# The q parts of a batch spread over three partition blocks: one transfer with the repetition outermost, or three transfers of 24 rows

## The reference, cut to what matters

```
q, k, v = heads of x @ W + b              # 8 batches, 16 heads, 512 rows, 8 dims
scores  = q @ k.T (* scale, + causal mask or bias)
p       = softmax(scores)
out     = (p @ v) joined over heads @ Wo + bo
```

## Time and profile before

| | us |
|---|---|
| median of 3 runs | 3335.12 |
| the runs | 3351.07, 3335.12, 3327.49 |
| span of the profiled execution | 3373.5 |
| TensorE busy in it | 2663.6 |
| layer 0's attention | about 0 to 620 |
| layer 0's experts and layer 1 | 620 to 1840 |
| layer 2 | 1840 to 2510 |
| layer 3 | 2510 to 3373.5 |

### The profile page before, as it was taken

The page is one execution under the profiler, slowest core; times in us unless marked ns, Lnnn a source line. Parts: engine busy times, 40 slices in busy tenths (PEclk is TensorE's granted clock), DMA queues, the critical chain, the costliest instruction groups (busy, mean ns, idle before and its releaser), DMA issues. The chain is left out here.

```text
span 3373.5 us, 52446 instructions
## 1 busy us (share of the span) xinstructions
PE 2663.6 (79%) x16466; PEld 1658.5 (49%) x16466; DVE 1628.8 (48%) x4008; ACT 1230.2 (36%) x2253; POOL 579.8 (17%) x594
## 2 busy tenths in 40 slices
PE   3777777788884788888888587877876888888887
PEld 1344444487772556556677243333443444444443
DVE  5566566400002444434423666666645555555553
ACT  1333333444443222222122244444432454444554
POOL 4322222000005433333100311111000000000000
PEclk7888888999996777777989698899888999999999
DMA  3112211266662000000054111111112011110111
GB/s 106 55 52 62 67 64 58 80 194 186 193 190 62 19 17 16 18 16 14 4 172 154 47 53 50 50 50 49 40 41 58 20 41 42 44 40 23 31 38 31
DMA packets 117431, 214.47 MB, mean 64 GB/s; under 512 B 21000, under 2 KB 90160, under 8 KB 110256
## 3 DMA queue, kind: packets, MB, share of 16 engines
q1 hardware_dynamic: 104048, 186.88, 18.5%
q0 software_dynamic: 10240, 20.99, 2.2%
q10 hardware_dynamic: 2880, 3.28, 0.3%
HBM read 158.50 MB, written 51.40 MB: 62 GB/s over the span
## 5 line engine op out<-in xcount | busy, mean ns | idle before, releaser
L525 DVE TENSOR_REDUCE arena<-bank 128x1 f32<-128x512 f32 (+3 forms) x1216 | 752.5, 658 | 221.7 <-PE bank L515 95.7
L501 PE MATMUL bank<-arena 125*128 125x512 bf16 (+3 forms) x1536 | 487.6, 357 | 174.1 <-DVE arena L525 107.1
L594 ACT ACTIVATE arena<-bank 128x512 f32<-128x512 f32 x640 | 378.9, 596 | 570.8 <-PE bank L584 506.6
L572 PE MATMUL bank<-arena 128*128 128x512 bf16 (+3 forms) x1536 | 469.1, 348 | 62.6 <-DMA arena<-arena 46.3
L594 ACT ACTIVATE arena<-bank,arena 128x512 f32<-128x512 f32 x512 | 343.3, 687 | 358.3 <-PE bank L572 249.0
L501 PEld LDWEIGHTS bank<-arena 125*128 125x128 bf16 x1536 | 146.2, 104 | 458.7 <-DVE arena L525 293.3
L609 PE MATMUL bank<-arena 128*32 128x512 f32 (+3 forms) x3072 | 318.8, 508 | 45.4 <-ACT arena L594 33.2
L572 PEld LDWEIGHTS bank<-arena 128*128 128x128 bf16 x1536 | 136.0, 103 | 285.3 <-ACT arena L594 130.5
L617 DVE COPY arena<-bank 128x512 f32<-128x512 f32 x96 | 66.4, 692 | 341.2 <-PE bank L609 330.8
L1023 POOL DMA_INDIRECT back_rows<-sorted_out,back_now x160 | 154.1, 963 | 404.1 <-issue 358.1
L1881 DVE TENSOR_TENSOR arena<-bank,arena 128x512 f32<-128x512 f32 (+3 forms) x256 | 109.8, 484 | 211.4 <-PE bank L1741 205.5
(11 more groups left out here) (250 smaller groups left out, 3667.9 us busy)
## 6 DMA issues: line engine op xcount, KB each, us to landing
arena<-in_L_ffn_w SPq DMA_DIRECT2D x80, 578.0 KB, 4.0
arena<-k_parts SPq DMA_DIRECT2D x48, 576.0 KB
arena<-q_parts SPq DMA_DIRECT2D x48, 576.0 KB
arena<-in_L_ffn_w SPq DMA_DIRECT2D x24, 768.0 KB, 4.5
arena<-sorted_in SPq DMA_DIRECT2D x104, 128.0 KB, 2.5
sorted_out<-arena SPq DMA_DIRECT2D x104, 128.0 KB, 4.1
k_parts<-arena SPq DMA_DIRECT2D x24, 384.0 KB
q_parts<-arena SPq DMA_DIRECT2D x72, 128.0 KB
```

Of the source, the lines that this page charges most:

```text
L501: ins = pe.matmul(mx[:, k * w:(k + 1) * w], Qx[0:KMAX, h, q * P:(q + 1) * P], Kx[0:KMAX, h, 0:w], start=(k == 0 or not L.causal), stop=not ...
L525: dve.reduce_max(L.mx[:, g % 2, q, heads[0]:heads[-1] + 1], mx[:, 0:w * len(heads)].rearrange("p (j k) -> p j k", k=w), AX.X).then_inc(L.m ...
L572: ins = pe.matmul(st[:, c:c + w], Kx[:, h, kb * P:(kb + 1) * P], Qx[:, h, T - w:T], start=(c == 0), stop=not (L.causal or far), skip_group ...
L594: act.activation(L.probs[:, n % L.PR, 0:w], st[:, 0:w], ACT.Exp, scale=L.scale).then_inc(L.st_free.sem, 1)
```

## The change

The spread of q is written as three transfers, each of the 24 rows of `q_parts` into one block of 24 partitions. They are issued in succession on the same queue, and each adds 16 to the semaphore, so that it counts 48 a batch and half. Bytes, rows and destinations are the same.

```diff
-            L.qx = [s(f"q_expanded{i}_", 16, 1) for i in range(HALVES)]
+            L.qx = [s(f"q_expanded{i}_", 16 * NPART, 1) for i in range(HALVES)]
...
-            q_rows = L.qd.rearrange("d i (o h) t -> o (d i) h t", o=1)
+            q_rows = L.qd.rearrange("d i h t -> (d i) h t")
...
-                sp.dma_start(copy_of(L.Qx, b)[0:KROWS, heads, :], q_rows[:, :, heads, :].rearrange(
-                    "o r h t -> o r (h t)").to_broadcast([NPART, NPART * HD, H * T // HALVES])).then_inc(L.qx[half].sem, 16)
+                for j in range(NPART):
+                    rows = slice(j * NPART * HD, (j + 1) * NPART * HD)
+                    sp.dma_start(copy_of(L.Qx, b)[rows, heads, :], q_rows[:, heads, :]).then_inc(L.qx[half].sem, 16)
...
-                pe.wait_ge(L.qx[half].sem, L.qx[half].at(b, 16))
+                pe.wait_ge(L.qx[half].sem, L.qx[half].at(b, 16 * NPART))
```

## The result

The changed kernel takes 3373.41 us in the median of five runs against 3342.77 us for the kernel before in the same call: a ratio of 1.0103 [1.0074, 1.0132], 1% slower. Measured again in another call it gave 1.0094 [1.006, 1.0128] (3399.65 against 3366.84). The prediction was 3320 us, a little faster; both its direction and its range were wrong.

A forecast was written before the change was run, and what follows sets the result against it. TensorE, busy 79% of the span, was taken as the bound, so only its waits count. Terms of -6.5 - 7.3 - 10 + 6 + 3 = -15 us from a 3335 us median gave 3320 us, range 3265 to 3352.

The forecast's parts named there:

- (1) Engines and rate: q's spread: twelve engines in place of three, 180 GB/s, no tail; whole spread 13.1 us in place of 23.
- The lower bound of 127: Low end of q's rate on twelve engines, in GB/s: spread 18.6 us, 0.77 us a row.
- (2) More issues on SP's queue: SP's queue: three issues per half in place of one, 2.4 us more per batch, costed at nothing.
- (3) Openings: First wait for q in layers 0 and 3: shorter by 6.5 us and 7.3 us.
- (4) Layer 2: Layer 2: waits for q and most for row stores go, together 12.3 us, taken as -10.
- (5) Row stores of layers 0 and 3: Loops of layers 0 and 3: stores land after 2.3 us plus 12.4 rows at 0.55 us; +6 and +3 us.
- Twelve engines in each other's way: Slower rival: q at 127 GB/s, row stores of layers 0 and 3 later; +40, 3375 us, chance 0.10.
- The row stores stop waiting: Faster rival: row stores pass early, waits in loops of layers 0 and 3 go; -63, 3272 us, chance 0.28.

The follow-up runs named there:

- the first hold: Changed kernel, next batch's spread held until group 2's row store landed: 3320.0 us, 0.9871; same wait in the kernel before: 3354.34 us, 0.9965.
- both holds: Changed kernel, spread's first half held for group 2's row store, second for group 3's: 3293.05 us, 0.9762; same in the kernel before: 3283.68 us, 0.9829.
- quarters: Changed kernel with both holds, and HALVES = 4 so each group of heads has its own transfers and semaphore: 3253.35 us, 0.9732.

## Why the prediction was wrong

**(1) Engines and rate: this step failed.** Twelve engines and no tail were right. The rate was not, where it counts: I took 180 GB/s, from windows in which k's transfer had the engines, and the stretch in which q's pieces run went at 138 in layer 0 and 144 in layer 3, in the mean of eight spreads each (at 169 in layer 2, near my figure). The two transfers differ in something that I did not weigh: k's spread reads each of its 24 rows for three partitions in a single transfer, q's pieces read the same 24 rows in three transfers, which follow one another within microseconds on twelve engines. With rows of their own the pieces reach 173 and 163, and as one transfer of 72 rows, q passes my 180: 197 and 193. Why layer 2 is faster than the other two with the same pieces stays open. The whole spread takes 15 us rather than 13, since k's share is still fast (213 GB/s), but the slow stretch is where the row store has to pass. The lower bound of 127 lay above the slowest spreads (115, 117 and 124); I had called the window it came from a mix and given the case a tenth.

The Trainium skill ("SBUF — State Buffer", "Door 1: The DMA port swizzle") had given an estimate of 163 GB/s for 24 partitions. The traces neither bear that number out nor refute it: the mean is 150 with the same source rows and 171 with separate ones, into the same 24 partitions, so a figure that goes by the partitions alone does not tell the two apart. The eight ports that I gave k's transfer beside it were a slip: by the same table partitions 0 to 71 reach ten.

**(2) More issues on SP's queue cost nothing: right.** Three take 1.35 us in place of one of 0.7, and the second k is issued 0.6 us later relative to the first. Nothing in the waits answers to that.

**(3) Openings.** Layer 0: forecast -6.5, measured -2.8 (15.66 to 12.86); layer 3: -7.3, measured -5.8 (16.03 to 10.21). The mechanism is right, and both are smaller, as the lower rate of step 1 has it; layer 0's is under the low end that I gave (-3.8). The difference between the two is scatter: over the eight openings of this form (the changed kernel, the pieces in the openings only, the first hold and both holds) TensorE starts 10.0 to 12.9 us after k's issue, 11.9 in the mean, and never as early as the 9.0 of the forecast.

**(4) Layer 2.** Forecast -10, measured -12.1 (13.6 to 1.5). The stretch became 26.7 us shorter, more than its waits; its granted clock is 0.92 in place of 0.89 in the two profiled executions. One pair does not show whether that belongs to the change.

**(5) Row stores of layers 0 and 3.** Forecast +6 and +3, measured +25.0 and +19.4. This is the term of the sum that was mis-sized: +9 where it was +44. That the store waits for some 12 rows of 8 KB held; the size was off by the time of a row, 0.55 us in the forecast and 0.70 at the 140 GB/s of the two loops. With that the formula gives 2.3 + 12.4 x 0.70 = 11.0 us, and 11.3 was measured in the mean. The count is not a law: with rows of 4 KB it is some 18.

The waits sum to -2.8 - 5.8 - 12.1 + 25.0 + 19.4 = +23.7 us, against -15. The timed differences are 31 and 34 us (0.0094 of 3367, 0.0103 of 3343), that of the profiled spans 15.6. The same untouched stretch from layer 0's last store to layer 2's first spread took 1228, 1241, 1243 and 1245 us in four profiled executions (the first hold, before, both holds, after), and from 1219 to 1254 us over the profiled executions of all the kernels shown here, so a single profile is uncertain by more than these differ. Whether the 8 to 10 us between waits and times are such scatter or a cost of the lower clock behind longer waits stays open.

**The rivals.** "Twelve engines in each other's way" has the mechanism of layers 0 and 3. That its 3375 us meets the measured 3373.41 is in part luck: its terms sum to +40 and the measured waits to +23.7 (openings -8.6 and -8.4 in its working, layer 2 -12.1 and -1.3, stores +44 and +50), and it started from a median of 3335 that further runs put at 3343. "The row stores stop waiting" fell: a store waits for some 13 rows where q comes in pieces of two rows per engine, and for as many where it comes as one transfer of six. By the rule of the Trainium skill that I had set beside it ("DMA: Bandwidth & Descriptors", "Queues, rings and completion order") smaller pieces could have let it through; the changed kernel's trace does not agree, since here its stores took longer (11.3 us, where they took 7.8 and 8.5 in the mean before).

## What to carry to other kernels

Before a bulk transfer is spread over more engines, look for the small transfer that shares them and is waited for: in this kernel it waited for some 12 or 13 rows of 8 KB, on three engines (12.4 in layer 2 before) as on twelve, so that it pays whenever a row gets slower. Order the bulk transfer behind the small one first; against the kernel before, that order gave 1.7% without the studied change, 2.4% together with it and 2.7% with quarters as well. And take the rate of a transfer from one of the same form, with the same pattern at its source and the same number of partitions, and from the mean of many windows rather than from one.

## What the runs showed of the hardware

In the six microseconds in which the pieces of q run, twelve engines that read the same 24 rows of memory three times carried 150 GB/s in the mean of 24 spreads (115 to 182), 171 from separate rows, and 196 as one transfer into 72 partitions; three engines alone had carried 78 to 80. A row store of 12 KB issued on another queue into layer 0's spreads took 11.3 us in the mean behind pieces of q at 141 GB/s, 8.8 where q came as one transfer, at 198, which is some 13 rows of 8 KB in both, and 8.0 behind rows of 4 KB at 163, some 18 of them; undisturbed it took 2.4.

With both stores kept out, waits that went away gave back more than themselves: with the pieces the waits fall by 57.7 us (85.3 to 27.6) and the time by 77 (3370.08 to 3293.05), with the single transfer by 35.7 and 58.3, with quarters by 67.7 (85.3 to 17.6) and 88.6. The other experiments do not show this surplus: there the time fell by 12 us less than the waits up to 14 more (first hold 38.8 us of waits and 46.8 of time with the pieces, 18.2 and 12.5 with the single transfer; rows of half the length 27.9 and 29.2). In layer 0 the windows show TensorE's clock beside that, first before, then with quarters:

```profile
113.00:127.00 14.00, 9.65 (x70) 4.89 (x69) 5.00 (x17) 2.39 (x4) 0.00 (x0) 0.74 0.43 110
```

```profile
113.00:127.00 14.00, 12.33 (x104) 5.95 (x104) 10.41 (x23) 7.16 (x13) 5.80 (x7) 1.00 0.54 133
```

The granted clock is 1.00 in this stretch in place of 0.74, and over 110:580 it is 0.92 in place of 0.88. Whether the clock accounts for the extra, or for any part of it, was not tested by itself.
